# Two evictions of the first expert matmul on ScalarE in place of one and a cast on VectorE

## The chip, the cores and the metric

The kernel runs on one core of one Trainium2 chip. A time is the device time of one execution in microseconds (us); less is better. The core has a matrix engine (TensorE, PE in the profile), a vector engine (VectorE, DVE), a scalar engine (ScalarE, ACT) and a general one (GpSimd, POOL), each with its own queue of instructions that it works off in order, and SyncE (SP), which issues transfers here. An engine waits for another through semaphores: a counter that the other raises when an instruction is done.

## The reference

The inputs are 8 sequences of 512 tokens with 128 features. The reference is a block in three parts: an encoder layer (half added), a segmented attention, and the encoder layer again. The encoder layer is convolution, attention with 16 heads of 8 features, layer norm, and a mixture of 8 experts in which every token goes through every expert:

```python
x = layernorm(x + attn_out, ln1_g, ln1_b)
probs = jax.nn.softmax(x @ gate_w + gate_b, axis=-1)
h = jax.nn.relu(jnp.einsum('bsd,edf->bsef', x, w1) + b1)     # 128 -> 512 in each expert
y = jnp.einsum('bsef,efd->bsed', h, w2) + b2                 # 512 -> 128
moe_out = jnp.einsum('bse,bsed->bsd', probs, y)
x = layernorm(x + moe_out, ln2_g, ln2_b)
```

The change touches how `h` comes from the first expert matmul into the second.

## The kernel before

An encoder layer of one sequence is a *unit*; there are 16 (8 sequences, twice), and eight shorter "mid" blocks for the segmented attention between them. Activations lie transposed, 128 features by 512 tokens, so one tile of 128x512 fills one bank of PSUM.

The order of all work is written out by hand on a grid of *ticks*. An iteration has 64 ticks. Each unit has its own clock `T`, and two to three units overlap: `walk` goes through the ticks of an iteration, and within a tick through the units from the oldest to the youngest. Each engine has its own `tick` function, which says what it issues at which `T` and what it waits for. A unit's steps:

- T = -43 to -7: normalisation of the input, convolution, queries, keys and values. On ACT this evicts `ch` and `conv` (L559, L561), then `q_parts` and `k_parts`; on DVE it makes `cl` (L820) and `rest` (L827).
- T = 0 to 63: one score matmul a tick for the row maxima (`score1a` and `score1b` in turn, L1014), and a maximum on DVE for each (`negmax`, L743). A score matmul waits until the maximum of two ticks before is done, since it overwrites its bank.
- T = 24 to 87: a second score matmul a tick (L1007) and an exponential on ACT for each (`probs`, L595). Every fourth tick four context matmuls (`ctx_ps`, L1027).
- T = 94 to 111: output projection, sum, layer norm (`x1n`, four pieces on DVE, L703), `x1h` and `x1l` (L604, L786).
- T = 112 to 181: the experts. There are 32 hidden tiles n = 0 to 31 in a unit (8 experts of 4), one every two ticks. A matmul here is made of three in a reduced-precision form (`fp32r`): both operands are split into a high part, rounded to fp32r, and the low rest, and high x high, low x high and high x low are summed in PSUM (L899, L900, L903 of the helper `three`).

A hidden tile n goes this way: PE computes `hid_ps` at even T; ACT adds the bias, applies relu and writes it in float32 to `hid` (two buffers, L619); DVE casts `hid` to the rounded `hidh` one tick later (a ring of four, L714); POOL subtracts, `hidl = hid - hidh` (L496); six ticks after its first matmul PE uses `hidh` and `hidl` in the second one, `y_ps` (L1052). After four tiles DVE multiplies `y_ps` by the gate (`gated`, L725), and POOL adds it up (`yacc`, L504). There is one bank `hid_ps`: PE's matmul for tile n + 1 waits on `h_full`, that ACT has written `hid` of tile n.

In the last part of the program nothing else is left to overlap (`alone`): there DVE does the subtraction too (L717), and the bank of `score1a` serves as a second hidden bank.

Of the kernel before, what the change touches and what calls it, by code (L numbers as in the profile page):

```python
# [7 lines left out]
ALU = mybir.AluOpType  # L8
ACT = mybir.ActivationFunctionType
AX = mybir.AxisListType  # L10
F32 = mybir.dt.float32
# [30 lines left out]
RING = 4  # L42
# [15 lines left out]
def wait(eng, sem, value):  # L58

    if isinstance(value, int) and value <= 0:  # L60
        return
    eng.wait_ge(sem, value)


def macaron(nc, x, Wq, bq, Wk, bk, Wv, bv, Wo, bo, conv_w, conv_b, wqkv, bqkv, wo, bo2, ln1_g, ln1_b,
            gate_w, gate_b, w1, b1, w2, b2, ln2_g, ln2_b, out):
    with ExitStack() as ctx:
        def sb(name, shape, dt=F32):
            return ctx.enter_context(nc.sbuf_tensor(name, shape, dt))
# [61 lines left out]
        hid = sb("hid", [128, 2, S])  # L131
        hidh, hidl = sb("hidh", [128, RING, S], F32R), sb("hidl", [128, RING, S], F32R)
# [31 lines left out]
        s = {}  # L164
# [19 lines left out]
        def col(k):  # L184
            return cols[:, k:k + 1]
# [9 lines left out]
        def chunks(tile):  # L195
            return tile[:].rearrange("p (c d) -> p c d", c=TC)
# [53 lines left out]
        def staged(k):  # L250


            return gate_b128[:, k % GATE_RING, :], s["ld_w"][k % GATE_RING], 16 * (k // GATE_RING + 1)

        def split_of(k):

            if k < E:
                return [w[:, k * FF:(k + 1) * FF] for w in (w1h, w1l)]
            return [w[:, (k - E) * FC:(k - E + 1) * FC, :].rearrange("p f d -> p (f d)") for w in (w2h, w2l)]
# [5 lines left out]
        def alone(u, n):  # L265

            return isinstance(u.n, int) and u.n * E * FC + n >= FIRST_ALONE

        def hid_bank(u, n):

            return score1[0] if alone(u, n) and n % 2 else hid_ps

        def wait_lo(eng, u, k):

            if alone(u, k - 1):
                wait(eng, s["h_lo_alone"], u.n * E * FC + k - FIRST_ALONE)
            else:
                wait(eng, s["h_lo"], u.count(32, k))
# [144 lines left out]
        def _(pool):  # L423
# [7 lines left out]
            def load_expert(k):  # L431
                src = w1[k] if k < E else w2[k - E].rearrange("(f p) d -> p f d", p=128)
                dst, loaded, _ = staged(k)
                if k >= E:
                    dst = dst.rearrange("p (f d) -> p f d", f=FC)
                if k >= GATE_RING:
                    pool.wait_ge(s["set_wl"], k + 1 - GATE_RING)
                pool.dma_start(dst, src).then_inc(loaded, 16)
# [31 lines left out]
            def tick(T, u, t, i, i0):  # L470

                if i0 == 0 and T == t and t % SPLIT_EVERY == 0:
                    k = t // SPLIT_EVERY
                    high, low = split_of(k)
                    pool.wait_ge(s["set_wh"], k + 1)
                    pool.tensor_tensor(low, staged(k)[0], high.bitcast(F32), ALU.subtract).then_inc(s["set_wl"], 1)
                if i0 == 0 and T == t and t % SPLIT_EVERY == 1 and t // SPLIT_EVERY + GATE_RING < 2 * E:
                    load_expert(t // SPLIT_EVERY + GATE_RING)
                if T == 22 - TICKS:
                    inv_std("f", u.n)  # L480
                    if i0 < 0:
                        set_up()
                for k, at in ((0, 39 - TICKS), (1, 42 - TICKS)):
                    if T == at:
                        wait(pool, s["f_p2"], u.count(2, k + 1))
                        pool.tensor_tensor(parts[k][:, 2, :], rest[:], parts[k][:, 1, :], ALU.subtract)\
                            .then_inc(s["f_p3"], 1)
                if T == 100:
                    inv_std("c", u.n)

                m = T - EXPERTS_AT - 1
                if 0 <= m < 64 and m % 2 == 0 and not alone(u, m // 2):
                    n = m // 2
                    wait(pool, s["h_hi"], u.count(32, n + 1))
                    wait(pool, s["y_mm"], u.count(32, n + 1 - RING))
                    pool.tensor_tensor(hidl[:, n % RING, :], hid[:, n % 2, :], hidh[:, n % RING, :].bitcast(F32),  # L496
                                       ALU.subtract).then_inc(s["h_lo"], 1)
                m = T - EXPERTS_AT - DOWN_LAG - 7
                if 0 <= m < 64 and m % 8 == 0:
                    e = m // 8  # L500
                    wait(pool, s["y_gated"], u.count(8, e + 1))
                    wait(pool, s["y_acc"], u.count(8, e))
                    ya = yacc[u.parity]
                    pool.tensor_tensor(ya[:], ya[:], gated[:], ALU.add).then_inc(s["y_acc"], 1)  # L504
                if T == 185:
                    inv_std("e", u.n)
                if T == 186:

                    wait(pool, s["e_in"], u.count(16, 16))
                    wait(pool, s["g2_half"], 2)  # L510
                    pool.tensor_tensor(chunks(resid), chunks(resid), b2_b[:].unsqueeze(1).to_broadcast([128, TC, D]),
                                       ALU.add).then_inc(s["e_zb"], 1)
                if T == 187 and i0 <= LAST_UNIT + 1:
                    end_block(pool, u)

            def mid(t, b, i, i0):
                if t == 3:
                    inv_std("m", b.n)
                if t == 32:
                    wait(pool, s["m_t"], b.count(1, 1))  # L520
                    wait(pool, s["m_in2"], b.count(16, 16))
                    pool.tensor_tensor(resid[:], resid[:], mq[:], ALU.add).then_inc(s["m_x"], 1)

            run(pool, lambda i, p, i0: walk(i, p, i0, tick, mid))


        @block.scalar
        def _(act):
# [10 lines left out]
            def tick(T, u, t, i, i0):  # L539
# [51 lines left out]
                if P2_AT <= T < P2_AT + 64:  # L591
                    n, j = divmod(T - P2_AT, HG)
# [21 lines left out]
                m = T - EXPERTS_AT  # L614
                if 0 <= m < 64 and m % 2 == 0:
                    n = m // 2
                    wait(act, s["h_mm"], u.count(32, n + 1))
                    wait_lo(act, u, n - 1)
                    act.activation(hid[:, n % 2, :], hid_bank(u, n)[:], ACT.Relu, bias=col(n))\  # L619
                        .then_inc(s["h_full"], 1)  # L620
# [28 lines left out]
        def _(dve):  # L649
# [57 lines left out]
            def tick(T, u, t, i, i0):  # L707

                m = T - EXPERTS_AT - 1
                if 0 <= m < 64 and m % 2 == 0:  # L710
                    n = m // 2
                    wait(dve, s["h_full"], u.count(32, n + 1))
                    wait(dve, s["y_mm"], u.count(32, n + 1 - RING))
                    dve.tensor_copy(hidh[:, n % RING, :], hid[:, n % 2, :]).then_inc(s["h_hi"], 1)  # L714
                    if alone(u, n):
                        wait(dve, s["h_hi"], u.count(32, n + 1))
                        dve.tensor_tensor(hidl[:, n % RING, :], hid[:, n % 2, :],  # L717
                                          hidh[:, n % RING, :].bitcast(F32), ALU.subtract).then_inc(s["h_lo_alone"], 1)
                m = T - EXPERTS_AT - DOWN_LAG - 6
                if 0 <= m < 64 and m % 8 == 0:  # L720
                    e = m // 8
# [388 lines left out]
```

## Time and profile before

| | us |
|---|---|
| median of 3 runs | 1839.16 |
| lowest, highest | 1838.27, 1841.56 |
| the profiled execution | 1839.75 |
| its span in the trace | 1838.0 |
| PE busy | 1721.2 (94%) |
| DVE busy | 1391.6 (76%) |
| ACT busy | 1082.7 (59%) |
| POOL busy | 966.4 (53%) |

The span is the time from the first to the last instruction in the trace, 1.75 us less than the device time of the same execution. Busy time is the time in which an engine worked on anything; PE's contains the overlap of matmuls that are pipelined, so that 94% leaves open how close PE is to its own limit. The granted clock of PE is 1.00 of full speed in the steady part of the program.

### The profile page before, as it was taken

The page shows a single profiled execution, that of the slowest core. Times are in us where ns is not written, and L with a number is a line of the kernel's source. Part 1 is how long each engine was busy: PE and PEld are TensorE (multiplying, and loading weights), DVE is VectorE, ACT ScalarE, POOL GpSimd, SP SyncE. Part 2 cuts the span into 40 slices and gives each one's busy share as a digit, 9 for nine tenths or more (in the row PEclk, how much of TensorE's full clock was granted, in tenths as well). Part 3 has the DMA queues.
Part 4 walks back from the last instruction along what each step waited for, and adds up shares of the span by engine and source line. Part 5 has one row for each costly group of instructions (what it writes and reads, how often), then busy time and mean ns, then how long its engine had stood idle before and what let it go on. Part 6 is the DMA issues. An engine that isn't in the chain of part 4 may idle for free.

```text
span 1838.0 us, 29109 instructions
## 1 busy us (share of the span) xinstructions
PE 1721.2 (94%) x8605; PEld 960.3 (52%) x8752; DVE 1391.6 (76%) x2967; ACT 1082.7 (59%) x1964; POOL 966.4 (53%) x829
## 2 busy tenths in 40 slices
PE   3888999999999999999999999999999999999977
PEld 1224555555555555555555555555555555555555
DVE  4777777776777788778787887778778777767787
ACT  2465666666666656666565665656656566665633
POOL 5312556565655656556564655656555565655232
PEclk7799999999999999999999999999999999999988
DMA  4311112021221212122121211212122121210111
GB/s 124 84 48 56 49 32 76 25 73 36 68 49 33 76 38 76 47 59 62 37 75 39 81 47 33 82 33 80 44 61 63 36 68 31 76 36 31 36 37 27
DMA packets 89773, 99.46 MB, mean 54 GB/s; under 512 B 14928, under 2 KB 65920, under 8 KB 89600
## 3 DMA queue, kind: packets, MB, share of 16 engines
q1 hardware_dynamic: 88336, 93.40, 18.3%
q0 software_dynamic: 1280, 4.20, 0.8%
q8 instruction: 71, 1.16, 0.3%
q14 instruction: 86, 0.70, 0.1%
HBM read 77.63 MB, written 20.19 MB: 53 GB/s over the span
## 4 chain that ended last, share of the span: by engine, by line
PE 73%; DVE 18%; issue 4%; ACT 2%; DMA 2%; SPq 1%; POOL 0%; DVEq 0%; ACTq 0%; POOLq 0%
PE ctx_ps L1027 11%; DVE negmax L743 6%; PE score1b L1014 5%; PE score1a L1014 5%; PE hid_ps L899 5%; PE y_ps L899 5%; PE hid_ps L903 5%; PE y_ps L903 5%; PE y_ps L900 5%; PE hid_ps L900 5%; PE score2b L1007 4%; PE score2a L1007 4%; DVE x1n L703 3%; DVE hidh L714 3%; PE misc L899 1%
## 5 line engine op out<-in xcount | busy, mean ns | idle before, releaser
L496 POOL TENSOR_TENSOR hidl<-hid,hidh 128x512 fp32r<-128x512 f32 x456 | 589.8, 1293 | 593.1 <-DVE hidh L714 581.3
L619 ACT ACTIVATE hid<-hid_ps,cols 128x512 f32<-128x512 f32 x484 | 333.0, 688 | 380.3 <-PE hid_ps L903 365.3
L743 DVE TENSOR_REDUCE negmax<-score1a 128x1 f32<-128x512 f32 x512 | 350.7, 685 | 208.9 <-PE score1a L1014 206.3
L595 ACT ACTIVATE probs<-score2a 128x512 f32<-128x512 f32 x512 | 305.1, 596 | 140.2 <-PE score2a L1007 80.4
L743 DVE TENSOR_REDUCE negmax<-score1b 128x1 f32<-128x512 f32 x512 | 349.3, 682 | 32.5 <-PE score1b L1014 30.9
L595 ACT ACTIVATE probs<-score2b 128x512 f32<-128x512 f32 x512 | 303.5, 593 | 24.5 <-PE score2b L1007 24.4
L1027 PE MATMUL ctx_ps<-probs,V 128*9 128x512 f32 x2048 | 269.2, 598 | 1.2
L899 PE MATMUL hid_ps<-x1h,w1h 128*128 128x512 f32 x484 | 258.3, 534 | 2.7 <-ACT x1h L604 2.7
L714 DVE CAST hidh<-hid 128x512 fp32r<-128x512 f32 x512 | 244.0, 477 | 12.8 <-ACT hid L619 12.3
L1014 PE MATMUL score1a<-Kp,Qp 96*128 96x512 bf16 x512 | 199.1, 389 | 29.1 <-DVE negmax L743 12.0
L1014 PE MATMUL score1b<-Kp,Qp 96*128 96x512 bf16 x512 | 199.4, 390 | 21.2 <-DVE negmax L743 18.9
L899 PE MATMUL y_ps<-hidh,w2h 128*128 128x512 f32 x512 | 211.0, 412 | 7.0 <-DVE gated L725 6.6
L504 POOL TENSOR_TENSOR yacc<-yacc,gated 128x512 f32<-128x512 f32 x128 | 164.9, 1288 | 77.4 <-DVE gated L725 77.4
L903 PE MATMUL y_ps<-hidl,w2h 128*128 128x512 f32 x512 | 203.8, 398 | 0.0
L900 PE MATMUL y_ps<-hidh,w2l 128*128 128x512 f32 x512 | 202.5, 395 | 0.0
L903 PE MATMUL hid_ps<-x1l,w1h 128*128 128x512 f32 x484 | 193.8, 400 | 1.6
L900 PE MATMUL hid_ps<-x1h,w1l 128*128 128x512 f32 x484 | 192.1, 397 | 0.0
L1007 PE MATMUL score2b<-Qp,Kp 128*128 128x512 bf16 x498 | 190.5, 382 | 0.8 <-ACT probs L595 0.4
L1007 PE MATMUL score2a<-Qp,Kp 128*128 128x512 bf16 x379 | 148.1, 391 | 3.7 <-DMA Qp<-m_parts 3.0
L899 PEld LDWEIGHTS hid_ps<-x1h,w1h 128*128 128x128 f32 x484 | 92.9, 192 | 81.9 <-issue 53.0
L1014 PEld LDWEIGHTS score1b<-Kp,Qp 96*128 96x128 bf16 x512 | 50.1, 98 | 146.2 <-DVE negmax L743 108.8
L899 PEld LDWEIGHTS y_ps<-hidh,w2h 128*128 128x128 f32 x512 | 97.0, 189 | 47.9 <-issue 18.5
(181 smaller groups left out, 2229.8 us busy)
## 6 DMA issues: line engine op xcount, KB each, us to landing
gate_b<-gate_dram SPq DMA_DIRECT2D x128, 256.0 KB, 3.7
q_parts_dram<-q_parts SPq DMA_DIRECT2D x48, 128.0 KB, 2.3
k_parts_dram<-k_parts SPq DMA_DIRECT2D x48, 128.0 KB, 2.3
Qp<-q_parts_dram SPq DMA_DIRECT2D x64, 96.0 KB
Kp<-k_parts_dram SPq DMA_DIRECT2D x64, 96.0 KB
gate_b<-in_L_ffn_w POOLq DMA_DIRECT2D x16, 256.0 KB, 3.7
Qp<-q_parts_dram SPq DMA_DIRECT2D x64, 64.0 KB
Kp<-k_parts_dram SPq DMA_DIRECT2D x64, 64.0 KB
```

The lines of the kernel that those rows point to most:

```text
L496: pool.tensor_tensor(hidl[:, n % RING, :], hid[:, n % 2, :], hidh[:, n % RING, :].bitcast(F32), ALU.subtract).then_inc(s["h_lo"], 1)
L504: pool.tensor_tensor(ya[:], ya[:], gated[:], ALU.add).then_inc(s["y_acc"], 1)
L595: act.activation(probs[:, n % 2, j, :], score2[(T - P2_AT) % 2][:], ACT.Exp, scale=SCALE)\
L619: act.activation(hid[:, n % 2, :], hid_bank(u, n)[:], ACT.Relu, bias=col(n))\
L714: dve.tensor_copy(hidh[:, n % RING, :], hid[:, n % 2, :]).then_inc(s["h_hi"], 1)
L743: dve.tensor_reduce(negmax[:, g % 2, T % 16:T % 16 + 1], score1[T % 2][:], AX.X, ALU.max, negate=True).then_inc(s["a_max"], 1)
L899: pe.matmul(dst, hi, rhi, start=start, stop=False)
L900: pe.matmul(dst, lo, rhi, start=False, stop=False)
L903: return pe.matmul(dst, hi, rlo, start=False, stop=stop)
L1007: pe.matmul(score2[k % 2][:], Kp[:, g * HG + j, kc * 128:(kc + 1) * 128], Qp[:, g * HG + j, :], start=True, stop=True).then_inc(s["a_s2"], 1)
L1014: pe.matmul(score1[T % 2][:], Qp[0:SCORE_ROWS, h, qc * 128:(qc + 1) * 128], Kp[0:SCORE_ROWS, h, :], start=True, stop=True).then_inc(s["a_s ...
L1027: last = pe.matmul(ctx_ps[32 * j:32 * j + DH + 1, :], V[p][:, kc, g * HG + j, :], probs[:, n % 2, j, :], start=(kc == 0), stop=(kc == TC - 1))
```

## The change

ACT evicts the bank twice: first rounded, straight into the ring `hidh`, and then in float32 into `hid`, as before. It raises `h_hi` itself, and waits for the ring's slot (`y_mm`) that DVE waited for. The cast on DVE is gone; of DVE's part of the tick only the subtraction of the `alone` tiles is left. POOL's subtraction now waits on both semaphores, since `h_hi` no longer implies `h_full`. PE's code is the same: the next tile's matmul waits on `h_full`, which the second of the two evictions raises.

```diff
--- POOL, tick
                     wait(pool, s["h_hi"], u.count(32, n + 1))
+                    wait(pool, s["h_full"], u.count(32, n + 1))
                     wait(pool, s["y_mm"], u.count(32, n + 1 - RING))
--- ACT, tick
                     wait(act, s["h_mm"], u.count(32, n + 1))
+                    wait(act, s["y_mm"], u.count(32, n + 1 - RING))
+                    act.activation(hidh[:, n % RING, :], hid_bank(u, n)[:], ACT.Relu, bias=col(n))\
+                        .then_inc(s["h_hi"], 1)
                     wait_lo(act, u, n - 1)
                     act.activation(hid[:, n % 2, :], hid_bank(u, n)[:], ACT.Relu, bias=col(n))\
                         .then_inc(s["h_full"], 1)
--- DVE, tick
-                if 0 <= m < 64 and m % 2 == 0:
+                if 0 <= m < 64 and m % 2 == 0 and alone(u, m // 2):
                     n = m // 2
+                    wait(dve, s["y_mm"], u.count(32, n + 1 - RING))
+                    wait(dve, s["h_hi"], u.count(32, n + 1))
                     wait(dve, s["h_full"], u.count(32, n + 1))
-                    wait(dve, s["y_mm"], u.count(32, n + 1 - RING))
-                    dve.tensor_copy(hidh[:, n % RING, :], hid[:, n % 2, :]).then_inc(s["h_hi"], 1)
-                    if alone(u, n):
-                        wait(dve, s["h_hi"], u.count(32, n + 1))
-                        dve.tensor_tensor(hidl[:, n % RING, :], hid[:, n % 2, :],
-                                          hidh[:, n % RING, :].bitcast(F32), ALU.subtract).then_inc(s["h_lo_alone"], 1)
+                    dve.tensor_tensor(hidl[:, n % RING, :], hid[:, n % 2, :],
+                                      hidh[:, n % RING, :].bitcast(F32), ALU.subtract).then_inc(s["h_lo_alone"], 1)
```

In the changed kernel the two evictions are L620 and L623, and lines behind them are two to four higher.

DVE's queue where the convolution of a young unit (`cl`), the layer norm of the middle one (`x1n`) and the experts of the oldest meet, before:

```order
L820 SCALAR_TENSOR_TENSOR cl<-misc,cols,ch 128x512 [waits f_c]
L714 CAST hidh<-hid 128x512 [waits y_mm,h_full]
L743 TENSOR_REDUCE negmax<-score1b 128x1 [waits a_s1]
L703 TENSOR_SCALAR x1n<-x1n,c_mv,c_ve 128x128 [waits c_rs]
L703 TENSOR_SCALAR x1n<-x1n,c_mv,c_ve 128x128 x3
L743 TENSOR_REDUCE negmax<-score1a 128x1 [waits a_s1]
L827 SCALAR_TENSOR_TENSOR rest<-misc,cols,q_parts 128x512 [waits f_p3,f_p1]
L714 CAST hidh<-hid 128x512 [waits y_mm,h_full]
L743 TENSOR_REDUCE negmax<-score1b 128x1 [waits a_s1]
```

and now, where the two casts have gone from between them and nothing else has moved:

```order
L822 SCALAR_TENSOR_TENSOR cl<-misc,cols,ch 128x512 [waits f_c]
L745 TENSOR_REDUCE negmax<-score1b 128x1 [waits a_s1]
L707 TENSOR_SCALAR x1n<-x1n,c_mv,c_ve 128x128 [waits c_rs]
L707 TENSOR_SCALAR x1n<-x1n,c_mv,c_ve 128x128 x3
L745 TENSOR_REDUCE negmax<-score1a 128x1 [waits a_s1]
L829 SCALAR_TENSOR_TENSOR rest<-misc,cols,q_parts 128x512 [waits f_p3,f_p1]
L745 TENSOR_REDUCE negmax<-score1b 128x1 [waits a_s1]
```

ACT's queue at the end of a unit's expert work, where the next unit's `x1h` follows, before:

```order
L619 ACTIVATE hid<-hid_ps,cols 128x512 [waits h_lo,h_mm]
L595 ACTIVATE probs<-score2a 128x512 [waits a_pv,a_s2]
L595 ACTIVATE probs<-score2b 128x512 [waits a_pv,a_s2]
L619 ACTIVATE hid<-hid_ps,cols 128x512 [waits h_lo,h_mm]
L604 ACTIVATE x1h<-misc,cols 128x512 [waits h_mm,c_x1f]
L595 ACTIVATE probs<-score2a 128x512 [waits a_pv,a_s2]
```

and now, where `x1h` and the exponentials stand behind one more eviction each time:

```order
L620 ACTIVATE hidh<-hid_ps,cols 128x512 [waits y_mm,h_mm]
L623 ACTIVATE hid<-hid_ps,cols 128x512 [waits h_lo]
L596 ACTIVATE probs<-score2a 128x512 [waits a_pv,a_s2]
L596 ACTIVATE probs<-score2b 128x512 [waits a_pv,a_s2]
L620 ACTIVATE hidh<-hid_ps,cols 128x512 [waits y_mm,h_mm]
L623 ACTIVATE hid<-hid_ps,cols 128x512 [waits h_lo]
L605 ACTIVATE x1h<-misc,cols 128x512 [waits h_mm,c_x1f]
L596 ACTIVATE probs<-score2a 128x512 [waits a_pv,a_s2]
```

## Rows read from the trace of the kernel before

**Rows 1.** The page: engines' busy us (share) xinstructions; shares of the last-ending chain.

```profile
PE 1721.2 (94%) x8605; PEld 960.3 (52%) x8752; DVE 1391.6 (76%) x2967; ACT 1082.7 (59%) x1964; POOL 966.4 (53%) x829
...
PE 73%; DVE 18%; issue 4%; ACT 2%; DMA 2%; SPq 1%; POOL 0%; DVEq 0%; ACTq 0%; POOLq 0%
```

**Rows 2.** Busy us and (instructions) in 805 to 916 us, with clock, DMA, GB/s.

```profile
805.00:916.00 111.00, 107.78 (x550) 61.12 (x560) 87.55 (x192) 68.07 (x125) 63.74 (x55) 1.00 0.20 56
```

**Rows 3.** PE's waits from 165 to 1676 us: us in total, times, longest.

```profile
PE score1b L1014 <- DVE negmax L743: 16.3, 23, 1.2
PE misc L991 <- DVE gate L804: 4.8, 13, 0.5
PE score1a L1014 <- DVE negmax L743: 4.8, 21, 0.4
```

**Rows 4.** The page, groups: busy us, mean ns, idle before and its releaser.

```profile
L714 DVE CAST hidh<-hid 128x512 fp32r<-128x512 f32 x512 | 244.0, 477 | 12.8 <-ACT hid L619 12.3
```

**Rows 5.** Timeline 894 to 906 us: start, length, instruction, idle before it.

```profile
894.56 0.69 ACT L619 ACTIVATE hid<-hid_ps,cols 128x512 f32<-128x512 f32 x1 [0.27 <-PE hid_ps L903]
...
...
896.54 1.02 POOL L468 TENSOR_TENSOR c_ve<-c_ve,minus_half 128x4 f32<-128x4 f32 x1
...
899.78 0.42 DVE L714 CAST hidh<-hid 128x512 fp32r<-128x512 f32 x1
...
900.27 1.28 POOL L496 TENSOR_TENSOR hidl<-hid,hidh 128x512 fp32r<-128x512 f32 x1 [2.72 <-DVE hidh L714]
900.71 2.68 DVE L703 TENSOR_SCALAR x1n<-x1n,c_mv,c_ve 128x128 f32<-128x128 f32 x4
...
904.57 0.41 DVE L714 CAST hidh<-hid 128x512 fp32r<-128x512 f32 x1
...
905.64 0.39 PE L1014 MATMUL score1b<-Kp,Qp 96*128 96x512 bf16 x1 [0.98 <-DVE negmax L743]
```

**Rows 6.** Timeline: a cast beside POOL, and one normalisation piece away from it.

```profile
826.97 1.29 POOL L284 TENSOR_TENSOR x1n<-x1n,g_b 128x512 f32<-128x512 f32 x1 [0.93 <-DVE x1n L703]
827.41 1.13 DVE L714 CAST hidh<-hid 128x512 fp32r<-128x512 f32 x1
...
875.75 0.33 DVE L703 TENSOR_SCALAR f_xn<-f_xn,f_mv,f_ve 128x128 f32<-128x128 f32 x1
```

**Rows 7.** Timeline: two evictions of one bank on ACT, one behind the other.

```profile
897.81 0.69 ACT L559 ACTIVATE ch<-misc,cols 128x512 fp32r<-128x512 f32 x1 [1.72 <-PE misc L903]
898.40 0.68 ACT L561 ACTIVATE conv<-misc,cols 128x512 f32<-128x512 f32 x1
```

**Rows 8.** Timeline: first and last of the 100 tight pairs, ACT and PE.

```profile
177.19 0.69 ACT L619 ACTIVATE hid<-hid_ps,cols 128x512 f32<-128x512 f32 x1
178.80 0.39 PE L900 MATMUL hid_ps<-x1h,w1l 128*128 128x512 f32 x1
...
1703.03 0.69 ACT L619 ACTIVATE hid<-hid_ps,cols 128x512 f32<-128x512 f32 x1 [2.32 <-PE hid_ps L903]
1704.64 0.39 PE L900 MATMUL hid_ps<-x1h,w1l 128*128 128x512 f32 x1
```

**Rows 9.** Timeline, drain: a hand-over from DVE to a waiting PE.

```profile
1789.62 0.75 DVE L725 SCALAR_TENSOR_TENSOR gated<-y_ps,cols,gate_b 128x512 f32<-128x512 f32 x1 [0.22 <-PE y_ps L903]
1790.52 0.47 PE L899 MATMUL y_ps<-hidh,w2h 128*128 128x512 f32 x1 [0.24 <-DVE gated L725]
1790.82 0.39 PE L900 MATMUL y_ps<-hidh,w2l 128*128 128x512 f32 x1
```

**Rows 10.** Timeline: x1h on ACT and x1l on DVE before an expert block.

```profile
804.99 0.77 ACT L604 ACTIVATE x1h<-misc,cols 128x512 fp32r<-128x512 f32 x1
806.48 0.68 DVE L786 TENSOR_TENSOR x1l<-yacc,x1h 128x512 fp32r<-128x512 f32 x1
```

**Rows 11.** Timeline, last subtractions of the drain.

```profile
1820.74 1.41 POOL L504 TENSOR_TENSOR yacc<-yacc,gated 128x512 f32<-128x512 f32 x1 [4.66 <-DVE gated L725]
1821.02 1.66 DVE L717 TENSOR_TENSOR hidl<-hid,hidh 128x512 fp32r<-128x512 f32 x1
```

## The prediction

> **What bounds the kernel now.** I read the engines' busy time and the shares of the last-ending chain first [rows 1]. TensorE (PE) is busy 94% and is 73% of the chain; VectorE (DVE) is busy 76% and is 18% of it; ScalarE (ACT) is busy 59% and is 2%. So the kernel runs at PE's pace, and a change on the other engines is worth only what PE waits for them. One row for a whole image (a unit of 111 us) says the same: PE 107.8 busy, DVE 87.6, ACT 68.1, POOL 63.7 [rows 2]. A busy PE is not a PE without delay, so I then read what PE waited for in the steady stretch, 165 to 1676 us: 16.3 + 4.8 us for the row maxima (negmax) and 4.8 us for the gate, all DVE work, together **25.9 us** [rows 3]. That is the whole sum that a lighter DVE can win there, however much work leaves it. No exponential and no eviction of a hidden tile by ACT is among the items of that list.
>
> **What is removed: 512 casts on DVE.** One takes 477 ns on average, 244 us in all [rows 4]. Off the path this is worth nothing. On the path it is worth this:
>
> - The largest stop of PE in a unit is 0.98 us in front of a score1b matmul [rows 5]; with the shorter stop in front of the score1a matmul just ahead of it, about 1.2 us. Read back from it on DVE: a cast at 904.57, before it a normalisation of x1n in four pieces that took 2.68 us, before that a cast at 899.78. From the start of each cast to the next instruction's start is 0.33 us, so the casts alone are 0.66 us of the stop. The normalisation is slow for another reason. One such piece, away from POOL's work, takes 0.33 us [rows 6], four should take 1.3; here POOL's subtraction hidl runs from 900.27 to 901.55, into the middle of it. In [rows 6] a cast begins at 827.41 while POOL works from 826.97 to 828.26, and it lasts 1.13 instead of 0.42 us: DVE's work from SBUF to SBUF stood still until POOL was through. POOL was that late because it waited for the cast, and the cast stood in DVE's queue behind cl, though ACT had evicted that hidden tile from 894.56 to 895.25 [rows 5]. After the change POOL has both inputs some 0.6 us after 895.25, does its subtraction as soon as the small POOL operation ahead of it ends (897.56), and is out of the way before the normalisation begins at about 900.4. So both parts of the stop go: 1.2 us in each of 14 units, 17 us, with a floor of 14 x 0.66 = 9 us if POOL collides again.
> - The other 9 us of the 25.9 are short waits (0.16 to 0.36 us), most with one cast ahead of the awaited DVE work. A shift of 0.33 us takes most of them: 7 us, between 3 and 9.
>
> Sum for the steady stretch: **24 us**, between 12 and 26. What is late next: nothing on DVE; PE's own rows.
>
> **What is added: a second eviction on ACT.** Both evictions read the same bank. The pair of evictions of another bank shows the price: the one to rounded fp32r takes 0.69 us, the one to float32 behind it 0.68, and it starts 0.59 after the first [rows 7]; so each of the 512 passes adds **0.59 us** to ACT's queue. ACT's busy time becomes 1082.7 + 512 x 0.69 = 1436 us, 78% of the span, and in a unit 68.1 + 32 x 0.69 = 90 of 111 us. There is room, so I price no pace of ACT, but two delays:
>
> - The hidden bank is released 0.59 us later, since PE's next first expert matmul still waits for the float32 tile. Queued behind that wait are all of PE's matmuls. I measured for 482 evictions how long after their end the next such matmul starts: for 100 it is under 0.65 us (nearly all 0.50 or 0.51), for 52 more it is under 1.1. First and last of the 100 are in [rows 8]: from ACT's start to PE's second matmul 1.61 us in both. After the change the release comes 0.59 + 0.69 = 1.28 us after ACT's start. From a release to the second matmul behind it took 0.45 us in the drain, where PE really stood waiting (1790.37 to 1790.82) [rows 9]. That makes 1.73 against 1.61: 0.12 us late, 100 times, **12 us**. With a slower hand-over it is more, up to the whole 0.59 (59 us); nothing excludes that it is hidden (0). I take 12 since the 0.45 is the same hand-over on the same engine. No gain is possible here.
> - The exponentials, the ctxT eviction and x1h come up to 0.59 us later. PE did not wait for an exponential in the steady stretch [rows 3], and ACT has free time in every unit, so I take 0 for these. At the beginning of an expert block x1h (804.99) would start 0.59 later and end at 806.35; x1l, which needs it, started at 806.48 [rows 10] with a cast directly ahead of it that is now gone. The two cancel: 0, between -2 and +3 us in all.
>
> The new wait of ACT (the ring slot must have been read by the second matmul of four tiles before) stands in front of the exponentials, but PE issues that matmul before the one whose result ACT evicts, so it is always over: 0. POOL's added wait for the float32 tile ends about 0.6 us after that for the rounded one; POOL was busy only 53% of the time [rows 1], and its result is used three steps later: 0.
>
> **The drain.** There both the cast and the subtraction are on DVE. Per expert PE stands some 0.24 us for gated [rows 9], which has only y_ps ahead of it: unchanged. The last subtractions are different: one at 1821.02 collides with POOL (1820.74) and takes 1.66 us [rows 11]; x1l, an operation of the same shape, took 0.68 [rows 10]. Without the cast it starts ahead of POOL, and the end comes some 0.9 us earlier. Three or four chains of small steps between 1745 and 1783 us lose a cast of 0.33 to 0.42 each. Together 3 us, between 0 and 4. In the fill no expert work runs: 0.
>
> **Sum.** 24 + 3 - 12 = 15 us less. Against the profiled execution's 1839.75: 1824.75. The median of the runs is 0.6 us below that execution, so I say **1824 us**, 0.8% faster.
>
> **The rivals.**
>
> 1. *The bank, slower than before.* The longer hold costs more than 0.12 us in a tight pair, because the fresh weights are loaded only after the release, or because more pairs become tight once PE stops less. Each 0.1 us is 10 us. From 0.31 us a pair (27 + 4 us over 100 pairs) it is slower than before; at the whole 0.59: 1839.75 + 59 - 27 = 1872. For it: 100 pairs have only 0.50 us of slack, less than the 0.59 added. Against it: part of the start is a weight load that overlaps the score matmul ahead. Chance 0.11.
> 2. *ACT's passes are dearer than the ones saved.* Each pass costs ACT 0.59 where it cost DVE 0.33; if those 0.26 us came onto the path each time, 512 x 0.26 = 133 us and 1973 us. Against it: ACT has 21 us free in each unit even afterwards. Chance 0.02. The Trainium skill, "ScalarE: Activation LUTs", section "Rules for kernel authors", tells to use VectorE and not ScalarE for relu, add and the like; by that rule this change goes the wrong way. The rows agree on the price of a pass, not on what it does to the time.
> 3. *POOL collides again, no change.* The normalisation still meets the next subtraction, the casts' own 0.33 us are all that is won: 12 + 2 - 12, so about 1838 us. For it: POOL's work is as long as before and only moves. Chance 0.12 for everything within 4 us, and 0.15 for a part gain (1829 to 1835).
> 4. *More.* The tight pairs cost nothing: 26 + 4 us, 1810. Chance 0.10.
>
> That the change does less than it says is excluded: in the order of instructions every cast is gone and every eviction is there twice.
>
> **How the numbers follow.** The forecast with sums between 1817 and 1829 has 0.50; with the part gain and rival 4, faster than the median by over 0.2% has 0.75; within 0.2% (3.7 us, about what a measurement of this kernel can tell from no change) 0.12; slower 0.13. The range goes from 1812 (rival 4 nearly whole) to 1840 (rival 3 whole), and leaves out 0.04 below and 0.14 above.
>
> **What would show it.** Right: PE's wait for negmax in front of score1b is near 0 in the steady stretch; the normalisation of x1n takes about 1.4 us at the place of [rows 5]; 512 more ACT rows of 0.69 us; from the rounded eviction's start to PE's second matmul about 1.73 us in tight pairs. Wrong: a new idle row of PE in front of hid_ps that ACT ends, or PE waiting for probs (rivals 1 and 2); a normalisation that still takes over 2 us (rival 3).

## The result, and the profile after

| | before | changed |
|---|---|---|
| median, runs of the same call (us) | 1840.42 (6 runs) | **1848.39** (6 runs, 1844.57 to 1851.11) |
| ratio to before | | **1.0045**, 95% interval 1.0033 to 1.0057 |
| span of the profiled execution (us) | 1838.0 | 1846.6 |

The prediction was 1824 us. The changed kernel is 8.3 us *slower*, outside the range and on its other side. Below, "us against before" is always the ratio less one, times 1839.

The page of the changed kernel, busy time and the shares of the last-ending chain, answers to [rows 1]:

```profile
PE 1718.8 (93%) x8605; PEld 947.4 (51%) x8752; DVE 1235.3 (67%) x2455; ACT 1329.5 (72%) x2476; POOL 963.7 (52%) x829
...
PE 76%; DVE 13%; issue 4%; ACT 4%; DMA 2%; SPq 1%; POOL 0%; ACTq 0%; DVEq 0%; POOLq 0%
```

DVE's busy time fell by 156 us, though 244 us of casts went. About half of the difference was never there to win: a cast of 0.42 us and the next instruction start 0.33 us apart, so part of each cast overlapped what stood behind it. With the lengths of all instructions added up one by one, DVE lost 205 us, and 39 came back in other instructions. Which ones, the groups by line of the changed kernel tell (busy us, mean ns | idle before). The first four are on DVE: `m_parts` belongs to the row maxima, `m_xn` to a mid block, `x1n` and `x1l` to a unit's step from attention to experts. The last is POOL's subtraction:

```profile
L755 DVE TENSOR_TENSOR m_parts<-m_rest,m_parts 16x128 bf16<-16x128 f32 x64 | 47.6, 744 | 19.3 <-ACT m_parts L585 17.7
L707 DVE TENSOR_SCALAR m_xn<-m_xn,m_mv,m_ve 128x128 f32<-128x128 f32 x32 | 22.3, 756 | 0.0
L707 DVE TENSOR_SCALAR x1n<-x1n,c_mv,c_ve 128x128 f32<-128x128 f32 x64 | 19.8, 374 | 0.2 <-POOL c_ve L468 0.2
L788 DVE TENSOR_TENSOR x1l<-yacc,x1h 128x512 fp32r<-128x512 f32 x16 | 19.2, 1202 | 1.9 <-ACT x1h L605 0.2
...
L497 POOL TENSOR_TENSOR hidl<-hid,hidh 128x512 fp32r<-128x512 f32 x456 | 588.1, 1294 | 480.1 <-ACT hid L623 262.5 <-ACT hidh L620 213.1 <-issue 3.9
```

The same groups in the kernel before:

```profile
L703 DVE TENSOR_SCALAR x1n<-x1n,c_mv,c_ve 128x128 f32<-128x128 f32 x64 | 40.7, 696 | 0.0
...
L753 DVE TENSOR_TENSOR m_parts<-m_rest,m_parts 16x128 bf16<-16x128 f32 x64 | 17.2, 268 | 7.0 <-ACT m_parts L584 7.0
...
L786 DVE TENSOR_TENSOR x1l<-yacc,x1h 128x512 fp32r<-128x512 f32 x16 | 10.9, 683 | 0.2 <-ACT x1h L604 0.2
L703 DVE TENSOR_SCALAR m_xn<-m_xn,m_mv,m_ve 128x128 f32<-128x128 f32 x32 | 8.9, 341 | 0.0
L496 POOL TENSOR_TENSOR hidl<-hid,hidh 128x512 fp32r<-128x512 f32 x456 | 589.8, 1293 | 593.1 <-DVE hidh L714 581.3 <-PE y_ps L903 11.8
```

None of these instructions was edited. `x1n` (the layer norm ahead of the experts, which runs where a young unit's convolution does) became fast, as predicted: 696 to 374 ns. But `m_parts` went from 268 to 744, `m_xn` from 341 to 756, `x1l` from 683 to 1202 ns. A second instruction of the mid block, the product `m_xn<-m_xn,mwt` (eight times), went from 1106 to 1600 ns. POOL's subtraction is as long as it was (1293, 1294 ns) and what released it is different: DVE's cast before, ACT's eviction now. From the end of ACT's float32 eviction to POOL's start it was 2.09 us in the median before, and it is 0.13 us now.

What PE waits for in 165 to 1676 us (total, times, longest) answers to [rows 3]:

```profile
PE score1b L1016 <- DVE negmax L745: 15.1, 29, 0.7
PE misc L993 <- DVE gate L806: 9.8, 13, 0.8
PE hid_ps L905 <- DVE x1l L788: 7.4, 13, 0.6
PE score1a L1016 <- DVE negmax L745: 7.3, 14, 1.5
PE misc L1078 <- ACT ctxT L601: 2.2, 8, 0.3
```

Only the waits in front of score1b fell, and by little: 16.3 to 15.1 us, in 29 waits in place of 23, the longest 0.7 in place of 1.2 us. Those in front of score1a rose from 4.8 to 7.3 us, the gate's doubled, and x1l is new. Three places of the timeline (start, length, instruction, idle before) show the pattern:

```profile
812.30 1.30 POOL L497 TENSOR_TENSOR hidl<-hid,hidh 128x512 fp32r<-128x512 f32 x1 [0.28 <-ACT hid L623]
...
812.87 1.28 DVE L788 TENSOR_TENSOR x1l<-yacc,x1h 128x512 fp32r<-128x512 f32 x1
...
814.20 0.50 PE L905 MATMUL hid_ps<-x1l,w1h 128*128 128x512 f32 x1 [0.57 <-DVE x1l L788]
...
820.60 1.28 POOL L497 TENSOR_TENSOR hidl<-hid,hidh 128x512 fp32r<-128x512 f32 x1 [3.18 <-ACT hidh L620]
...
820.68 1.34 DVE L755 TENSOR_TENSOR m_parts<-m_rest,m_parts 16x128 bf16<-16x128 f32 x1 [0.34 <-ACT m_parts L585]
...
822.67 0.39 PE L1016 MATMUL score1b<-Kp,Qp 96*128 96x512 bf16 x1 [0.51 <-DVE negmax L745]
...
847.94 2.52 POOL L497 TENSOR_TENSOR hidl<-hid,hidh 128x512 fp32r<-128x512 f32 x2
...
849.52 2.79 DVE L707 TENSOR_SCALAR m_xn<-m_xn,m_mv,m_ve 128x128 f32<-128x128 f32 x4
...
852.97 0.39 PE L1016 MATMUL score1b<-Kp,Qp 96*128 96x512 bf16 x1 [0.71 <-DVE negmax L745]
```

Each time a DVE instruction that reads SBUF begins while POOL subtracts, and ends only after POOL is through: the small `m_parts` (0.27 us by itself) at 822.02, that is 0.14 us after POOL's end at 821.88. The four pieces of `m_xn` meet two operations of POOL, the subtraction until 850.46 and the sum `yacc` behind it, 850.41 to 851.72. Of 64 `m_parts`, none began inside a POOL subtraction before and 34 do now; of 16 `x1l`, none before and 14 now; of the 8 blocks of `m_xn`, none before and all 8 now. The 8 products `m_xn<-m_xn,mwt` begin inside one as well, and none did before.

Why the old kernel was spared is in [rows 5] and in the order: the cast itself was the thing that released POOL, and behind a cast DVE's next instruction is `negmax` in 414 of 512 cases, which reads PSUM and takes 0.68 us beside POOL or not. A cast on DVE kept POOL's work out of the stretches in which DVE had SBUF work to do. Without it POOL starts when ACT is ready, wherever DVE happens to be.

The Trainium skill states such a rule in "SBUF — State Buffer", section "Who interferes with whom": a DVE instruction with two SBUF inputs contends with a GpSimd instruction that reads SBUF, and one in a mode with two ports contends with GpSimd too; the one that issues first blocks the other fully, and `tensor_reduce` never contends on trn2. The rows agree: x1l, with two inputs in SBUF, went from 683 to 1202 ns and ended 0.55 us after POOL each time it began inside a subtraction, and the means of negmax are 681 to 686 ns in both kernels.

For the path I lined up PE's second matmul of `hid_ps` (x1h, w1l) of all 512 hidden tiles, each kernel minus before. Lag in us since the start of unit 6, at tile n, and at the very last tile of the program (single executions; at the first tile of unit 0, behind the fill, they are already up to 4 us apart, and the last column contains that):

| kernel | n=1 | 3 | 12 | 21 | 29 | next unit | last tile |
|---|---|---|---|---|---|---|---|
| changed | 0.46 | 1.62 | 2.27 | 2.85 | 1.42 | 1.47 | +9.5 |
| e4 | 0.01 | 0.44 | 0.51 | 0.82 | 0.89 | 0.94 | +13.2 |
| e8 | -0.04 | 0.42 | 0.44 | 0.77 | 0.86 | 0.89 | +15.3 |
| e5 | -0.26 | -0.53 | -0.89 | -1.43 | -2.14 | -2.14 | -31.0 |
| e7 | -0.13 | -0.02 | -0.25 | -0.76 | -2.20 | -2.15 | -27.1 |
| e1 | -0.12 | 1.02 | 2.05 | 1.54 | 0.98 | 1.03 | -0.5 |
| e2 | -0.13 | 0.10 | -0.12 | -0.63 | -1.20 | -1.15 | -15.1 |
| e10 | -0.13 | -0.52 | -0.74 | -1.25 | -2.69 | -2.64 | -38.4 |
| e11 | 0.00 | -0.43 | -0.38 | -0.40 | -0.40 | -0.40 | -5.8 |

In the changed kernel x1l costs 0.46 us (n = 1), m_parts and the gate together 1.1 us (n = 3; e4 and e8, in which no `m_parts` is long, lose 0.4 us there), m_xn 0.9 us (n = 12, only where there is a mid block). At n = 29, the place of [rows 5], 1.4 us are won. At unit 14 the lag is 16.7 us; the drain gives 7 us back.

### The profile page after: what moved, and what is told of

Same layout as the page of the kernel before. It is cut to its first block, busy times and chain, and to the rows that moved or that the text cites. A ratio compares the mean times of both kernels' runs of the same rounds, so it can differ in the third digit from the quotient of the medians.

```text
span 1846.6 us, 28659 instructions
## 1 busy us (share of the span) xinstructions
PE 1718.8 (93%) x8605; PEld 947.4 (51%) x8752; DVE 1235.3 (67%) x2455; ACT 1329.5 (72%) x2476; POOL 963.7 (52%) x829
## 4 chain that ended last, share of the span: by engine, by line
PE 76%; DVE 13%; issue 4%; ACT 4%; DMA 2%; SPq 1%; POOL 0%; ACTq 0%; DVEq 0%; POOLq 0%
PE ctx_ps L1029 11%; PE hid_ps L901 6%; PE hid_ps L905 6%; PE score1a L1016 5%; PE y_ps L901 5%; PE score1b L1016 5%; PE hid_ps L902 5%; PE y_ps L905 5%; PE y_ps L902 5%; PE score2b L1009 5%; PE score2a L1009 4%; DVE negmax L745 3%; PE misc L967 2%; DVE gated L727 2%; PE misc L901 1%
## 5 line engine op out<-in xcount | busy, mean ns | idle before, releaser
L497 POOL TENSOR_TENSOR hidl<-hid,hidh 128x512 fp32r<-128x512 f32 x456 | 588.1, 1294 | 480.1 <-ACT hid L623 262.5
L620 ACT ACTIVATE hidh<-hid_ps,cols 128x512 fp32r<-128x512 f32 x484 | 334.3, 691 | 295.3 <-PE hid_ps L905 287.0
L596 ACT ACTIVATE probs<-score2a 128x512 f32<-128x512 f32 x512 | 307.1, 600 | 40.2 <-remote 26.8
L623 ACT ACTIVATE hid<-hid_ps,cols 128x512 f32<-128x512 f32 x484 | 331.6, 685 | 0.0
L596 ACT ACTIVATE probs<-score2b 128x512 f32<-128x512 f32 x512 | 308.1, 602 | 24.6 <-PE score2b L1009 24.0
L901 PE MATMUL hid_ps<-x1h,w1h 128*128 128x512 f32 x484 | 250.0, 516 | 2.0 <-ACT x1h L605 1.4
L1016 PE MATMUL score1a<-Kp,Qp 96*128 96x512 bf16 x512 | 199.0, 389 | 33.0 <-DVE negmax L745 14.5
```

The costliest lines, as they stand in the source:

```text
L596: act.activation(probs[:, n % 2, j, :], score2[(T - P2_AT) % 2][:], ACT.Exp, scale=SCALE)\
L620: act.activation(hidh[:, n % RING, :], hid_bank(u, n)[:], ACT.Relu, bias=col(n))\
L901: pe.matmul(dst, hi, rhi, start=start, stop=False)
L1016: pe.matmul(score1[T % 2][:], Qp[0:SCORE_ROWS, h, qc * 128:(qc + 1) * 128], Kp[0:SCORE_ROWS, h, :], start=True, stop=True).then_inc(s["a_s ...
```

## The experiments

| kernel | ratio to before, interval | us against before |
|---|---|---|
| e1 changed, POOL behind the maximum | 1.0006 (0.9997 to 1.0015) | +1.1 |
| e2 changed, marker on DVE | 0.9904 (0.9891 to 0.9918) | -17.7 |
| e3 before, drain as changed | 0.9958 (0.9944 to 0.9971) | -7.7 |
| e4 before, one more eviction | 1.0084 (1.0071 to 1.0097) | +15.4 |
| e5 before, casts of 8 columns | 0.9847 (0.9830 to 0.9864) | -28.1 |
| e6 before, subtraction of 8 columns | 0.9905 (0.9891 to 0.9920) | -17.5 |
| e7 changed, subtraction of 8 columns | 0.9841 (0.9826 to 0.9856) | -29.2 |
| e8 before, ACT pass without the bank | 1.0079 (1.0059 to 1.0098) | +14.5 |
| e9 = e2, last sum of a unit later | 0.9854 (0.9832 to 0.9877) | -26.8 |
| e10 = e9, no marker at tiles 26, 27 | 0.9781 (0.9761 to 0.9802) | -40.3 |
| e11 before, last sum of a unit later | 0.9962 (0.9942 to 0.9982) | -7.0 |

**The two sides apart: e5 and e4.** e5 is the kernel before with casts of 8 of 512 columns (the rest of `hidh` is a constant: the computation leaves it out). It tests what DVE's relief is worth with POOL's release left at its place.

```diff
-                    dve.tensor_copy(hidh[:, n % RING, :], hid[:, n % 2, :]).then_inc(s["h_hi"], 1)
+                    dve.tensor_copy(hidh[:, n % RING, 0:8], hid[:, n % 2, 0:8]).then_inc(s["h_hi"], 1)
```

> The kernel before, with each cast on 8 of 512 columns (the rest of the rounded tile keeps a constant, so that part of the computation is left out). DVE's relief alone: POOL still waits behind it at the same place, ACT does one eviction. The prediction's terms for the relief were 24 + 3 us: 1812 to 1816. If the waits of PE on DVE have other causes: 1830 or more.

e4 keeps the cast and adds only ACT's pass:

```diff
                     wait(act, s["h_mm"], u.count(32, n + 1))
+                    wait(act, s["h_spare"], u.count(32, n))
+                    act.activation(spare[:], hid_bank(u, n)[:], ACT.Relu, bias=col(n)).then_inc(s["h_spare"], 1)
                     wait_lo(act, u, n - 1)
```

> The kernel before with the cast kept, and one more eviction of the same bank on ACT into a buffer that nobody reads, ahead of the real one: ACT's cost alone. Collision theory: 114 tight pairs by 0.04 us and some later float32 tiles: 1841 to 1848. ACT theory: as late as the changed kernel or later, since nothing is saved on DVE: 1856 or more.

The relief alone gave 28.1 us, with 212 of 477 ns of each cast still there; the passes alone cost 15.4. That is between the two outcomes that had been named for e4 (1841 to 1848, and 1856 or more, against 1854.7 measured), so ACT's side costs more than the collision account had allowed it, and e8 below looks for the reason. Together that is a gain of 12.7 us where the change has a loss of 8.3: **21 us** are in neither half, give or take 4 to 5 by the three intervals. They come only when the cast is *gone*.

**Whether the missing part is POOL: e6 and e7.** Both shorten POOL's subtraction to 8 columns (the other columns of `hidl` are zero and left out of the result), once before the change and once after. With POOL's work of 0.21 us in place of 1.29 there is little to collide with.

```diff
-                    pool.tensor_tensor(hidl[:, n % RING, :], hid[:, n % 2, :], hidh[:, n % RING, :].bitcast(F32),
+                    pool.tensor_tensor(hidl[:, n % RING, 0:8], hid[:, n % 2, 0:8], hidh[:, n % RING, 0:8].bitcast(F32),
```

> The kernel before, with POOL's subtraction on 8 of 512 columns (the low parts stay 0 elsewhere: left out of the computation). Pairs with the next run. Collision theory: here too the collisions go (normalisation of x1n from 696 to about 350 ns), 1822 to 1834.

> The changed kernel, with the same short subtraction on POOL. Collision theory: without POOL's long operation the change no longer loses, x1l is at 690 and m_parts at 270 ns, and this is at least 3 us faster than the kernel before with the short subtraction. ACT theory: still at least 8 us slower than that one.

Between these two the change is worth 29.2 - 17.5 = 11.7 us of *gain*, what e4 and e5 add up to (12.7). With the long subtraction it is 8.3 us of loss. So the missing 20 us are shown to hang on the length of POOL's subtraction in the changed kernel. That they come from an earlier `hidl` is ruled out: in neither original kernel does PE wait for it. In e6 x1n fell from 696 to 517 ns only, not to the 350 expected, since POOL's sum `yacc` lies in it too. In e7 `m_parts` and `x1l` are back at their own length, and `m_xn`, which still meets `yacc`, is at 485 ns:

```profile
L756 DVE TENSOR_TENSOR m_parts<-m_rest,m_parts 16x128 bf16<-16x128 f32 x64 | 17.8, 278 | 19.4 <-ACT m_parts L585 17.8
...
L789 DVE TENSOR_TENSOR x1l<-yacc,x1h 128x512 fp32r<-128x512 f32 x16 | 11.1, 692 | 1.9 <-ACT x1h L605 0.2
```

**What ACT's passes cost by: e4 against e8.** The prediction's price was the bank, held longer. e8 puts the added pass behind the eviction, over a buffer in SBUF, so that the bank is free as early as before:

```diff
                         .then_inc(s["h_full"], 1)
+                    wait(act, s["h_spare"], u.count(32, n))
+                    wait(act, s["zero_v"], 1)
+                    act.activation(spare[:], spare[:], ACT.Relu, bias=col(n)).then_inc(s["h_spare"], 1)
```

> The kernel before with its cast, and one more ACT pass of 128x512 behind each eviction, from a buffer in SBUF into itself: it loads ACT's queue as the extra eviction did and does not hold the bank. The extra eviction cost 15.8 us. If the held bank was the cost (114 tight pairs by 0.04 us, 5 us, and more): 1840 to 1844. If the later queue behind it was (gate's exponential, x1h, later tiles): 1849 to 1853.

+14.5 against +15.4: the same within the intervals, which leave room for some 4 us either way. So the bank is at most a small part of the price; ACT's queue is the main one. In the lag table both kernels lose at two places, 0.4 us at n = 3 and 0.3 at n = 21. The first is PE's wait for the gate, which in e8 is the second item of its list for 165 to 1676 us, twice the 4.8 of [rows 3]:

```profile
PE misc L996 <- DVE gate L809: 9.6, 13, 0.7
```

The gate needs the exponential `eg` on ACT. From the start of DVE's last step ahead of it to its own start it took 1.62 us before and 2.19 in e4, which is one pass more ahead of it. The kernel before and then e4, timeline:

```profile
811.86 0.19 DVE L796 TENSOR_TENSOR lg<-lg,gmax 128x32 f32<-128x32 f32 x1
813.48 0.21 ACT L608 ACTIVATE eg<-lg 128x32 f32<-128x32 f32 x1
```

```profile
816.41 0.19 DVE L799 TENSOR_TENSOR lg<-lg,gmax 128x32 f32<-128x32 f32 x1
818.60 0.21 ACT L609 ACTIVATE eg<-lg 128x32 f32<-128x32 f32 x1
```

The second place (in unit 2 it is at n = 23) is a young unit's input, rounded on ACT (`xh`); then DVE makes the low rest `xl` from it out of the bank `misc`, and then PE may write that bank. Before, PE did not stand there; in e4 it does:

```profile
443.67 0.62 ACT L554 ACTIVATE xh<-misc 128x512 fp32r<-128x512 f32 x1
...
444.32 0.69 DVE L817 TENSOR_TENSOR xl<-misc,xh 128x512 fp32r<-128x512 f32 x1 [0.92 <-ACT xh L554]
...
445.07 0.42 PEld L968 LDWEIGHTS misc<-ident,ctxT 128*128 128x128 f32 x4 [0.57 <-DVE xl L817]
```

**The drain alone: e3.** The kernel before, with the change made only for the 56 `alone` tiles: ACT evicts twice, and their cast on DVE is gone (a line not shown here). ACT's part:

```diff
+                    if alone(u, n):
+                        wait(act, s["y_mm"], u.count(32, n + 1 - RING))
+                        wait(act, s["h_hi"], u.count(32, n))
+                        act.activation(hidh[:, n % RING, :], hid_bank(u, n)[:], ACT.Relu, bias=col(n))\
+                            .then_inc(s["h_hi"], 1)
```

> The kernel before, with the double eviction on ACT (and no cast) only for the last 56 tiles, where DVE does the subtraction too. By the two traces the changed kernel gains about 7 to 8 us behind 1677 us and loses 16 to 17 before. If that gain belongs to the drain alone: 1832 to 1835 us. If it was only caused by the shifted steady part: 1839 to 1842.

-7.7 us. By the lined-up tiles 6.7 us of it are won between 1742 and 1787 us (before's times), in steps of 0.4 to 1.7 us, with one step of 0.7 back, and nothing per tile behind that. The profiled span as a whole is 7.4 us shorter.

**Where to put POOL: e1 and e2.** If the position of POOL's subtraction is the cause, moving it back must cure the changed kernel, with the double eviction kept. e1 lets POOL wait for the row maximum of the same tick:

```diff
                     wait(pool, s["h_full"], u.count(32, n + 1))
+                    wait(pool, s["a_max"], u.count(64, T))
```

> The changed kernel, and POOL's subtraction also waits until DVE has done all row maxima of the ticks before, so that it starts beside a maximum from PSUM again, as it did behind the cast. Collision theory (the cast had kept POOL's subtraction out of DVE's work from SBUF): m_parts on DVE falls from 744 to about 270 ns, x1l from 1202 to about 690, the gain of 17 us that the changed kernel loses again in the steady part comes out: 1825 to 1836 us. ACT theory (the second eviction costs PE the time): nothing gained, 1845 to 1852.

+1.1 us: 7 of the 21 us, and above the 1825 to 1836 us that had been expected. x1l is well again, but the subtraction now starts 0.91 us behind ACT's eviction in the median (0.13 in the changed kernel) and meets others (groups by line, e1):

```profile
L708 DVE TENSOR_SCALAR f_xn<-f_xn,f_mv,f_ve 128x128 f32<-128x128 f32 x64 | 38.3, 765 | 1.5 <-POOL f_ve L468 1.5
L756 DVE TENSOR_TENSOR m_parts<-m_rest,m_parts 16x128 bf16<-16x128 f32 x64 | 33.7, 527 | 19.4 <-ACT m_parts L586 17.8
...
L708 DVE TENSOR_SCALAR m_xn<-m_xn,m_mv,m_ve 128x128 f32<-128x128 f32 x32 | 25.4, 854 | 0.0
...
L789 DVE TENSOR_TENSOR x1l<-yacc,x1h 128x512 fp32r<-128x512 f32 x16 | 11.1, 692 | 1.9 <-ACT x1h L606 0.2
```

f_xn is new there (559 ns before), and PE waits 8.2 us for it. e2 restores the old order: a tiny write on DVE stands where the cast stood, and POOL waits for it (1.24 us behind ACT's eviction in the median; the write itself, unlike the cast, doesn't wait for ACT):

```diff
--- DVE, tick, at the cast's old place
+                if 0 <= m < 64 and m % 2 == 0 and not alone(u, m // 2):
+                    wait(dve, s["h_mark"], u.count(32, m // 2))
+                    dve.memset(mark[:], 0.0).then_inc(s["h_mark"], 1)
--- POOL, tick
                     wait(pool, s["h_full"], u.count(32, n + 1))
+                    wait(pool, s["h_mark"], u.count(32, n + 1))
```

> The changed kernel with a tiny DVE operation (128x8, some 0.06 us) where the cast stood; POOL's subtraction waits for it. Collision theory: the order of POOL against DVE is nearly that of before, with 0.3 us less DVE work each time: 1823 to 1834 us, m_parts near 270 ns, x1n near 370 to 700. ACT theory: 1845 to 1852.

**-17.7 us against before, 26 us below the changed kernel**, for 456 instructions of 65 ns more on DVE. The marker runs and POOL starts behind it, in the shadow of a maximum (timeline of e2):

```profile
819.97 0.07 DVE L718 MEMSET mark<- 128x8 f32 x1
820.20 0.69 DVE L750 TENSOR_REDUCE negmax<-score1b 128x1 f32<-128x512 f32 x1 [0.17 <-PE score1b L1021]
820.28 1.29 POOL L499 TENSOR_TENSOR hidl<-hid,hidh 128x512 fp32r<-128x512 f32 x1 [1.43 <-DVE mark L718]
```

In the groups by line `m_parts` and `x1l` have the lengths that they have by themselves, while x1n and the gate are long, as in the kernel before:

```profile
L709 DVE TENSOR_SCALAR x1n<-x1n,c_mv,c_ve 128x128 f32<-128x128 f32 x64 | 43.4, 738 | 0.2 <-POOL c_ve L469 0.2
...
L811 DVE TENSOR_TENSOR gate<-eg,ginv 128x32 f32<-128x32 f32 x16 | 18.4, 1151 | 0.6
L760 DVE TENSOR_TENSOR m_parts<-m_rest,m_parts 16x128 bf16<-16x128 f32 x64 | 17.8, 279 | 19.4 <-ACT m_parts L587 17.8
...
L793 DVE TENSOR_TENSOR x1l<-yacc,x1h 128x512 fp32r<-128x512 f32 x16 | 11.1, 692 | 1.6 <-ACT x1h L607 0.2
```

**The two that were left: e9, e10, e11.** x1n collides as before the change, since the marker stands where the cast stood. And the gate, an operation of 128x32, takes 1.0 us in the mean in *both* original kernels, beside POOL's last sum of the unit ahead. e9 holds that sum back until the gate is done; e11 does the same to the kernel before.

```diff
                     wait(pool, s["y_acc"], u.count(8, e))
+                    if e == 7 and u.n + 1 < UNITS:
+                        wait(pool, s["c_pr"], u.n + 2)
```

> The changed kernel with the DVE marker of e2, and with one more wait on POOL: its last of the eight partial sums of y (yacc, e=7) starts only when DVE has done the first step of the next unit, so that it no longer runs beside DVE's gate product. Theory (what costs time is POOL's work in SBUF beside DVE's SBUF operations): the gate product falls from 1.02 us to the 0.2 to 0.4 us of its size, the 7.3 us that PE waits for it in e2 go, and the time is 1814 to 1818 us against 1821.5 of e2. Rival (the gate product is long by itself, and the wait comes from ACT's exponential ahead of it): it stays at 1.0 us and the time within 2 us of e2, or longer if the later sum delays POOL's next work.

> The kernel before (its cast kept) with the one wait that e9 adds to e2: POOL's last partial sum of y in a unit starts only when DVE's gate product is done. It tells whether that gain needs the changed kernel. Theory (the collision is there in both kernels): the gate product falls from 1.03 to about 0.22 us, the 4.8 us that PE waits for it go, and the time falls by 5 to 9 us, to 1830 to 1834 us. Rival (in the kernel before something else is as late, the negmax reductions behind it on DVE): within 2 us of 1839.

e10 also leaves the marker's wait out where the changed kernel was right, at the layer norm of x1n:

```diff
-                    wait(pool, s["h_mark"], u.count(32, n + 1))
+                    if n not in (26, 27):
+                        wait(pool, s["h_mark"], u.count(32, n + 1))
```

> e9 with the marker's wait left out for the two expert tiles at the place where the unit's first normalise is done (tiles 26 and 27, 14 units). Theory: e1 and the changed kernel have that normalise at 0.38 us in place of 0.74, and the changed kernel gained 1.34 us for each unit there where e2 gained 0.46; so 0.6 to 0.9 us for each of 14 units, 8 to 12 us off e9: 1803 to 1810 us. Rival (e2's marker costs nothing there, and the gain in the changed kernel was only a lag being made up): within 2 us of e9.

e9: 9.1 us below e2, where 4 to 7 had been expected. PE no longer waits for the gate in its steady stretch, though ACT's exponential comes as late as in e4 (2.18 us behind DVE's step): at this place the later exponential had cost PE time only together with the collision behind it. e11: -7.0, as expected; that gain was there without the change. e10: **-40.3 us, 1799.7 us against 1840.5 in the same call**, the fastest kernel here, 13.5 us below e9 where 8 to 12 were expected. Groups by line of e10:

```profile
L712 DVE TENSOR_SCALAR x1n<-x1n,c_mv,c_ve 128x128 f32<-128x128 f32 x64 | 19.8, 372 | 0.2 <-POOL c_ve L469 0.2
L763 DVE TENSOR_TENSOR m_parts<-m_rest,m_parts 16x128 bf16<-16x128 f32 x64 | 17.8, 279 | 19.4 <-ACT m_parts L590 17.8
...
L814 DVE TENSOR_TENSOR gate<-eg,ginv 128x32 f32<-128x32 f32 x16 | 3.5, 216 | 0.6
```

PE's longest waits in its steady stretch are these, and no DVE work of weight is among them:

```profile
PE misc L1086 <- ACT ctxT L606: 2.2, 8, 0.3
PE hid_ps L909 <- ACT x1h L610: 0.8, 1, 0.8
PE hid_ps L909 <- ACT hid L628: 0.6, 1, 0.6
PE score1b L1024 <- DVE negmax L753: 0.5, 1, 0.5
```

With POOL's work at good places the two evictions are worth 33 us (e10 against e11); at the places that fell out of the edit they cost 8.

## Why the prediction was wrong

- **What bounds the kernel: right.** PE sets the pace, and what DVE makes it wait for is the stock to win from. That stock was read as 25.9 us. Between the first tiles of units 0 and 14, the same stretch, e5 wins 26.1 us by the relief alone, and e10 wins 29.7 with ACT's passes in it. So the stock is a little larger than the list; where the rest lies was not looked into.
- **The stop at the layer norm of x1n: right.** 1.2 us in each unit was said, 1.34 measured at n = 29; the four pieces take 1.11 us (0.37 each) where 1.4 was said. The reading of why they were slow was half: behind the subtraction POOL's sum `yacc`, 901.52 to 902.80, lay in them too. In the changed kernel both are over before they begin.
- **"What is late next: nothing on DVE": the step that failed.** The working of [rows 5, 6] has the mechanism in full: an SBUF operation on DVE stands until POOL is through, and POOL starts behind the cast. From it I drew that POOL's subtraction moves out of the way at one place. It starts earlier behind ACT's eviction at 443 of 456 places, and I didn't go through the other DVE operations in SBUF to see which of them it now meets. Three rows, x1l, m_parts and m_xn, none longer before than by themselves, would have been the ones to check against the time at which ACT finishes. Price: the 20 to 21 us by which the change misses the sum of e4 and e5, and e7 less e6. Rival 3 had "POOL collides again", but at the old place only, which bounded it at no change.
- **POOL's added wait "ends 0.6 us after; its result is used three steps later: 0".** True of POOL's consumers, and beside the point. The wait that was *removed*, POOL's for the cast, was the one with a function. Nothing in PE's list showed that, because a wait that prevents a collision shows up as no wait at all.
- **The short waits, 7 us: not gained** in the changed kernel (score1b: the sum fell only from 16.3 to 15.1). In e5 this relief is there: 9.4 us are left of the 25.9.
- **The bank, 12 us: nearly the right size for the wrong reason.** From ACT's first eviction to PE's second matmul the tight pairs take 1.656 us in the mean of 114 after the change, 1.618 in 115 before: 0.04, not 0.12; some 4 us, and e4 less e8, the cost of the bank alone, is 0.9 us, nothing that the intervals would tell from zero.
- **"The exponentials, ctxT and x1h come up to 0.59 us later: 0": mis-sized.** ACT's queue costs 14.5 us (e8), about half of it at the gate, and that half only while the gate collides as well (e9). The reason given was that PE doesn't wait for an exponential in [rows 3]; but the gate's 4.8 us there *is* such a wait, a few short DVE steps removed: eg on ACT, the gate on DVE, then PE. A chain that ends in an awaited row has to be followed back to each engine that is made slower.
- **The drain, 3 us: mis-sized**, 7.7 (e3). It has many short chains of ACT, DVE and PE, and I counted four with one cast each; the steps are up to 1.7 us. The 0.9 us at the very end came as said (lag +9.5 at the last tile, +8.6 at the end of the span).
- **ACT's busy time "1436 us, 78%": too high**, 1329.5 us and 72%. Passes that start 0.59 us apart overlap, and the sum counted 0.69 us for each; no term of the forecast rests on it.

As a sum: relief of DVE -28.1 (e5, drain included; predicted -27), ACT's queue +15 (e4, e8; predicted +12), collisions at new places +21 (predicted 0; it is the rest of the sum here, and e6 and e7 give 20 by themselves). Two of three terms were right within 3 us, the second of them by luck: a bank that cost at most some 4 us was priced at nearly what the queue took. The third turned the sign.

What stays open: how the 21 us divide among the places beyond the single executions lined up above, the mid block's product `m_xn<-m_xn,mwt` among them, which no run takes by itself. e10 fits: 14 units of 0.87 us are 12 us, and its 13.5 below e9 differ from that by less than the intervals tell.

## What to carry to other kernels

When an instruction is taken away, ask not only who waited for it but who was *held back* by it: list the work it released, find when that work now starts, and look at what every engine that shares something with it does at that time. Here that pair is DVE and POOL, both in SBUF; POOL's operation of 1.3 us was best released, at most places, by a DVE instruction with PSUM work behind it, and a marker of 65 ns was a cheap way to do that (26 us below the changed kernel). A removed load is worth its gain only together with the position of what stays.

## What the runs showed of the hardware that I had not expected

- What a collision costs hangs on how much of POOL's operation is left, and not on the size of DVE's: 16x128 (0.27 us alone) took up to 1.35 us, 128x32 (0.19 us in e10) took 1.05 to 1.20 us, ending 0.14 and 0.05 us after POOL's 128x512 operation. Small steps on a path lose most in proportion.
- A cast of 128x8 takes 161 ns in the median where 128x512 takes 417 (the means, 212 and 477, contain collisions): a sixty-fourth of the columns leaves over a third of the time. A memset of 128x8 takes 65 ns.
- Two ACT passes over the same bank, the second behind the first, start 0.59 us apart at 0.69 us each (810.90 and 811.49 in the changed kernel), and PE's next matmul into the bank came only 0.04 us later for it on the tight pairs.
